# P times V of windowed attention in 128-row pieces against zero-padded copies of V

## What is computed

```python
def local_attention(q, k, v):          # 8 heads of 64, windows of 128 tokens
    bk, bv = look_around(bk), look_around(bv)      # window before and this one
    sim = einsum('bhwid,bhwjd->bhwij', bq, bk)
    mask = (i < j) | (i > j + WINDOW) | (j == -1)
    attn = softmax(where(mask, -max, sim))
    return einsum('bhwij,bhwjd->bhwid', attn, bv)
```

## Time and profile before

| | |
|---|---|
| median of 3 runs | 3594.43 us (3592.74 to 3596.29) |
| profiled execution: time | 3596.59 us |
| profiled execution: span, first to last instruction | 3594.7 us |
| mean granted TensorE clock | 0.96 of full speed |
| PE busy | 3213.7 us, 89% of the span |
| DVE, ACT, POOL busy | 66%, 47%, 41% |

### The profile page before, as it was taken

How to read it: one execution, slowest core, us unless ns; L and a number is a source line. 1 busy time by engine, 2 the same in 40 slices (tenths; PEclk the granted TensorE clock), 3 DMA queues, 4 the chain that set the end, 5 groups by cost and what they waited for, 6 DMA issues and landing times. The chain is left out here.

```text
span 3594.7 us, 98004 instructions
## 1 busy us (share of the span) xinstructions
PE 3213.7 (89%) x34660; PEld 2760.0 (77%) x34660; DVE 2373.7 (66%) x6692; ACT 1679.5 (47%) x4415; POOL 1458.4 (41%) x1500
## 2 busy tenths in 40 slices
PE   1999989989998998997999989979999894977779
PEld 0788868868886887885788868858888784866668
DVE  4666657666666775765666657666665675765566
ACT  1666652256665223543566652246666220531235
POOL 3766630066664002333766640066766000113220
PEclk9999999999999999997999999989999997998999
DMA  4111121021111101001111121021111111000001
GB/s 146 36 36 36 34 69 30 27 58 37 36 36 32 45 20 45 10 9 38 35 36 36 36 66 33 24 57 37 36 36 33 55 29 31 1 0 0 0 7 41
DMA packets 166769, 126.77 MB, mean 35 GB/s; under 512 B 23740, under 2 KB 146968, under 8 KB 166040
## 3 DMA queue, kind: packets, MB, share of 16 engines
q1 hardware_dynamic: 166552, 123.85, 12.7%
HBM read 48.29 MB, written 25.17 MB: 20 GB/s over the span
## 5 line engine op out<-in xcount | busy, mean ns | idle before, releaser
L2325 POOL TENSOR_TENSOR prob<-prob,rsum 128x384 f32<-128x384 f32 x512 | 416.1, 834 | 212.4 <-DVE rsum L1602 212.4
L1063 ACT ACTIVATE prob<-prob,nmax 128x192 f32<-128x192 f32 x1024 | 456.5, 454 | 7.5 <-DVE nmax L1595 7.5
L1223 ACT ACTIVATE gate<-bank,bias 128x512 f32<-128x512 f32 x192 | 132.4, 690 | 543.9 <-PE bank L287 543.8
L2312 POOL TENSOR_TENSOR rn<-ss,mhalf 128x16 f32<-128x16 f32 x128 | 375.0, 2930 | 10.6
L2293 POOL TENSOR_TENSOR rstd<-meanvar,eps 128x4 f32<-128x4 f32 x48 | 10.9, 228 | 906.2 <-DVE meanvar L1529 906.2
L285 PE MATMUL bank<-wqkv_hi,hT_hi 128*128 128x512 f32 x768 | 332.2, 433 | 17.3 <-DVE rot_t L1557 7.6
L1595 DVE CUSTOM_DVE_ANT_0 prob<-bank,masks,rn 128x192 f32<-128x192 f32 x768 | 274.6, 414 | 107.0 <-PE bank L423 106.1
L2319 POOL TENSOR_TENSOR qk<-rot_t 128x512 f32<-128x512 f32 x256 | 331.4, 1296 | 33.5 <-DVE ss L1569 33.5
L285 PE MATMUL bank<-gT_hi,w_hi 128*128 128x512 f32 x704 | 280.7, 399 | 32.4 <-DVE w_lo L1697 32.4
L287 PE MATMUL bank<-wqkv_hi,hT_lo 128*128 128x512 f32 x768 | 305.7, 398 | 0.0
L286 PE MATMUL bank<-wqkv_lo,hT_hi 128*128 128x512 f32 x768 | 305.4, 398 | 0.0
(11 more groups left out here) (269 smaller groups left out, 9620.1 us busy)
## 6 DMA issues: line engine op xcount, KB each, us to landing
Vswap<-V SPq DMA_DIRECT2D x256, 128.0 KB, 2.3
ya<-Y SPq DMA_DIRECT2D x40, 256.0 KB, 2.3
H<-Y SPq DMA_DIRECT2D x128, 64.0 KB, 1.8
H<-ya SPq DMA_DIRECT2D x128, 64.0 KB, 1.8
yb<-Y SPq DMA_DIRECT2D x128, 64.0 KB, 1.6
HB<-Y SPq DMA_DIRECT2D x32, 256.0 KB, 2.8
HB<-yb SPq DMA_DIRECT2D x32, 256.0 KB, 3.1
raw<-in_L_ffn_wqkv SPq DMA_DIRECT2D x4, 1536.0 KB, 6.6
```

The lines of the kernel that those rows point to most:

```text
L1063: ins = e.activation(pb, pb, ACT.Exp, bias=nm[r][:, x:x + 1], scale=-1.0, accum_out=sums[r][:, x:x + 1])
L2312: e.tensor_tensor(rn[u][:, :], ss[:, :], mhalf[:, :], ALU.pow).then_inc(s_plRN, 1)
L2325: e.tensor_tensor(pair, pair, rs[:, 2 * gi:2 * gi + 2].unsqueeze(2).to_broadcast([P, 2, KW]), ALU.mult).then_inc(s_plPN[gi], 1)
```

## The change

The diff, cut to its core (a wait count of the preparation goes from 3 to 4, and one from 4 to 3, in all five programs; the declarations of s_vs, s_peLF and Vs change to match):

```diff
-PAIRS = [(0, 2), (1, 3), (4, 6), (5, 7)]
+PAIRS = [(0, 4), (1, 5), (2, 6), (3, 7)]
...
+        Vleft = [[sb(f"V{n}{i}", [P, INNER]) for n in ("lo", "hi")] for i in range(2)]
...
-        Vs = [sb(f"Vswap{i}", [P, INNER]) for i in range(U)]
...
                     if hf == 0:
-                        e.wait_ge(s_vs[u % 2], 32 * ((G - u % 2) // 2 + 1) + OFF)
+                        e.wait_ge(s_vs[u], 64 * ((G - u) // U + 1) + OFF)
...
-                    e.sem_inc(s_passed, 1)
-                    lefts(hf, True)
-                    mains(hf, False)
-                    mains(1 - hf, True)
-                    e.wait_ge(s_peLF, 4 * G + 2 * hf + 2 + OFF)
-                    e.sem_inc(s_passed, 1)
-                    ins = lefts(1 - hf, False)
+                    for i in range(2):
+                        keys = (V[before_], V[u], Vleft[u % 2][0], Vleft[1 - u % 2][1])
+                        for x in range(4):
+                            for g in range(2):
+                                gi = 2 * hf + g
+                                h = PAIRS[gi][i]
+                                o0 = (h // 2) * P + DH * (x % 2)
+                                p0 = (i if x < 2 else 2) * P + DH * (x % 2)
+                                ins = e.matmul(bank[6][DH * (h % 2):DH * (h % 2) + DH, o0:o0 + DH], keys[x][:, h * DH:(h + 1) * DH], PTs[gi][:, p0:p0 + DH], start=x == 0, stop=x >= 2, skip_group_check=True)
...
+            for x in Vleft:
+                for y in x:
+                    i = e.memset(y[:, :], 0.0)
+            i.then_inc(s_prepV, 1)
...
-                e.memset(Vs[U - 1][:, :], 0.0).then_inc(s_prepB, 1)
-                prep['B'] += 1
...
                     e.wait_ge(s_acV, G + 1 + OFF)
-                    e.wait_ge(s_vs[u % 2], 32 * ((G - u % 2) // 2) + OFF)
-                    e.dma_start(Vs[u][0:DH, :], V[u][DH:P, :]).then_inc(s_vs[u % 2], 16)
-                    e.dma_start(Vs[u][DH:P, :], V[u][0:DH, :]).then_inc(s_vs[u % 2], 16)
+                    e.wait_ge(s_vs[u], 64 * ((G - u) // U) + OFF)
+                    e.wait_ge(s_pePV[0], G + OFF)
+                    e.wait_ge(s_pePV[1], G + OFF)
+                    for i in range(2):
+                        rr, cc = slice(DH * i, DH * i + DH), slice(4 * DH * i, 4 * DH * i + 4 * DH)
+                        for half_ in range(2):
+                            e.dma_start(Vleft[u % 2][half_][rr, cc], V[u][DH * half_:DH * half_ + DH, cc]).then_inc(s_vs[u], 16)
```

More of the change, by code:

```diff
@@ L235, in build @@
         s_stb = sem("s_stb")
-        s_vs = [sem(f"s_vs{i}") for i in range(2)]
-        s_peLF = sem("s_peLF")
+        s_vs = [sem(f"s_vs{i}") for i in range(U)]
         s_x = [sem(f"s_x{i}") for i in range(2)]
@@ L261, in build @@
         g_plBO = sem("g_plBO")
-        everything = [s_raw, s_raw2, s_small, s_prepA, s_prepB, s_prepV, s_prepP, s_stb, *s_vs, s_peLF, *s_x, *s_ld, *s_st,
+        everything = [s_raw, s_raw2, s_small, s_prepA, s_prepB, s_prepV, s_prepP, s_stb, *s_vs, *s_x, *s_ld, *s_st,
                       s_peHT, s_acHT, s_dvHT, s_peV, s_acV, s_plRN, *s_peQK, *s_acSQ, *s_dvRT, *s_dvSS, *s_plAD, s_dvQN, *s_peKT,
@@ L291, in tensor_program @@
             e.wait_ge(s_raw, prep['raw'] + OFF)
-            prep['V'] += 3
+            prep['V'] += 4
             e.wait_ge(s_prepV, prep['V'] + OFF)
@@ L318, in prep_A @@
                     prep['B'] += 2
-                prep['B'] += 4
+                prep['B'] += 3
                 e.wait_ge(s_prepA, prep['A'] + OFF)
@@ L1447, in vector_program @@
             prep['V'] += 1
+            for x in Vleft:
+                for y in x:
+                    i = e.memset(y[:, :], 0.0)
+            i.then_inc(s_prepV, 1)
+            prep['V'] += 1
             e.memset(zrow, 0.0).then_inc(s_prepV, 1)
@@ L2710, in pass_A @@
                 for x in s_vs:
-                    e.wait_ge(x, 16 * NT * (run + 1) + OFF)
+                    e.wait_ge(x, 64 * GRP * (run + 1) + OFF)
                 for x in s_st:
```

## The result

The changed kernel takes 4215.28 us (median of 4 runs, 4209.5 to 4217.46) against 3593.65 us (4 runs beside it): ratio 1.1726, 95% interval 1.1706 to 1.1746, slower by 17%. The profiled execution took 4217.46 us, with a span of 4215.7.

The account below looks back on a forecast made before the run. TensorE was taken to set the pace in the passes; -0.54 for P times V, +4.52 wait and +2.1 clock over 108 tiles, less 11 elsewhere, gave +646 on 3596.6, so 4240 us, range 4100 to 4360.

Parts of the forecast that it names:

- The main case: Whole kernel: P times V gains, but TensorE waits for H and its clock falls; 4240 us, chance 0.83.
- P times V: TensorE, each tile: four changes of row shape go, 0.13 us each, saving 0.54 us.
- the rival in which the 0.13 stays: P times V: 0.13 us belongs to each new operand block, so no gain and the waits come; 4309 us, chance 0.05.
- The wait: TensorE at ht: H's load, behind SP's copies, comes late; 6.42 against 1.90 us, so 4.52 idle, 108 times.
- semaphore to first issue: SP, from the end of P times V to the first copy's issue: 0.2 us.
- first copy to last load: SP's issues: two more copies, 1.16 us, plus 3.06 from first copy to second load with Y's store between.
- landing and wake-up: From the issue of H's second load until TensorE starts on it: 2.0 us.
- The clock: TensorE behind each wait: 8 us of lowered granted clock, costing 2.1 us a wait.
- The rival in which the clock holds: TensorE in the passes: the clock doesn't fall, only waits and the P times V gain count; 4014 us, chance 0.08.
- The sum: +6.08 us for each of 108 tiles with the wait, -11 for the other 20 together; total +646.
- The ends at 0: Pass and kernel starts: memset removed (0 to -2.1 us) and four DVE memsets added (0 to +2.1), together 0.
- Faster, because the load isn't late: SP's load of H lands within TensorE's 1.90 us, so only P times V's gain counts; 3525 us, chance 0.03.

Follow-up runs that it names:

- e6: Kernel before, with left products run over all 128 rows; pairs, copies and waits as before (it leaves the computation): 3519.15 us, ratio 0.9792.
- e4: e1 with TensorE's wait for itself put back in each half-step of P times V: 3519.47 us, ratio 0.9792.
- e1: Changed kernel with the copies of tile T moved from SP's slot T-1 to slot T, behind the load of H: 3522.24 us, ratio 0.9795.
- e3: Changed kernel with four buffers instead of two for V's last 64 rows, so copies wait for P times V one tile earlier: 3524.00 us, ratio 0.9799.
- e8: Kernel before plus the two waits for P times V ahead of its copies, store of Y moved ahead of them: 3988.47 us, ratio 1.1102.
- e5: Changed kernel with eight filler matmuls of constants per tile ahead of ht's wait for H: 4112.66 us, ratio 1.1441.

## Why the prediction was right

Forecast 4240 us, range 4100 to 4360; measured 4215. The main case held, each step at its place, though some of the closeness is luck: the largest term was 45 us too high, and the clock's was 12 too low.

- P times V: forecast -0.54 us a tile. The earlier trace rows has 2.59 us, after has 2.01: -0.58. The prediction gave each of five changes of shape the same 0.13; the four that went cost 0.14 to 0.16 each, and 2.01 less the prediction's 1.92 leaves 0.09 for the fifth, on leaving. e6 shows that the change of shape is the cause, which disposes of the rival in which the 0.13 stays; e4 shows that the self-wait was rightly put at nothing.
- The wait: forecast 4.52 us, measured 4.10 as the mean of the 108 waits ahead of L358, just under the lower bound of 4.13 (4.14 a slot by all idle time of PE in the third pass). Term by term on one slot: semaphore to first issue 0.09 (415.46 to 415.55) against 0.2; first copy to last load 4.24 against 1.16 + 3.06 = 4.22; landing and wake-up 1.83 against 2.0; together 6.16 against 6.42. The rest is TensorE's own work after P times V, which I had at 1.90 and which ends 2.04 later (415.46 to 417.50): before, `ht` had started inside the modelled end of the transposes ahead of it.
- The clock: forecast 2.1 us a wait, measured 2.21 by PE's busy time and 1.99 by filling the wait. The 8 us behind two waits show 0.64 and 0.79, where the prediction's rows had 0.62 and 0.80; over the whole kernel the mean is 0.90 against 0.91 forecast. The rival in which the clock holds asked for 1.00 in the pass; it was 0.87.
- The sum: forecast +6.08 a slot with a wait, +657 in all; the four passes have 5.74 and 620. The 37 us between them are the wait's term, 0.42 x 108 = 45 too high, with P times V gaining 4 more than forecast, less some 12 by which the clock's term was too low. Outside these slots I had put -11, the gain of the other 20 tiles; the profiled executions are 4217.46 - 3596.59 = 621 apart, so what came is +1. From `ht` of tile 0 to that of tile 4 the four passes take 127.5 us in both kernels: the gain of P times V doesn't show there. That makes the 25 us between forecast and result.
- The ends at 0: PE's first transpose of H starts at 73.7 us, 1.7 later than before, inside the bound of +2.1. The six kernels with four memsets on DVE ahead of SP's first weight loads have it at 73.7 to 74.9 us, the four without at 72.0 to 73.2, so the memsets are the likely cause; no run changes them alone.
- Faster, because the load isn't late: it was late every time (the shortest of the 108 idle times ahead of L358 is 3.1 us). e1 and e3 are what that case looks like once it is made true, at the 3525 us that it named (3522 and 3524).

## What to carry to other kernels

When a buffer is reused sooner, ask which queue the new wait stands in and what is listed behind it: the wait was harmless for the copies it guards and cost 17% through a load that has nothing to do with them. Move the wait's end by a buffer or the load ahead of it; either gave back everything here. And where TensorE sets the pace, count a repeated idle gap one and a half to one and two thirds times, for the half clock behind it: that is what gaps of 2.1 to 4.1 us in slots of 16.5 to 18.7 us cost here.

## What the runs showed that I had not expected

- The clock falls behind short waits too. With 2.10 us of idle time in a slot of 16.5 (e8), the granted clock over the stretch was 0.92 and PE's busy time rose by 1.41 us a slot; the expectation had left open whether it holds there. The half-speed level is 1.2 GHz.
- TensorE doing useless work in its wait is faster than TensorE idle: in the third pass of e5 1.99 us a slot.
- A loop body longer by 32 matmuls brought idle time that the profile puts down to "issue", 3.3 to 5.1 us at the start of five iterations of the first pass and two of the second (e5).
